# A state-space layer and an FP4 feed-forward layer on one core: x loaded in place, loop buffers laid over used weights, engine lists written out, Silu table loaded first

## The reference

```python
# block 1: linear state space, state of 16, hidden 256
xB = x @ B.T;  xD = x @ D.T
state_t = state_(t-1) @ A.T + xB_t          # a scan over 2048 steps
out = layernorm(states @ C.T + xD) * gamma + beta
x = layernorm(x + out)
# block 2: feed-forward, 256 -> 704 -> 256
q(v): per 16 values, scale = max|v| / 6, v / scale rounded to the FP4 grid, times scale
h = silu(q(x) @ q(w_gate).T) * (q(x) @ q(w_up).T)
x = layernorm(x + q(h) @ q(w_down).T)
```

## Time and profile before

| | |
|---|---|
| median of three runs | 607.63 us |
| the profiled execution | 608.48 us |
| its span in the trace | 606.7 us |
| TensorE busy | 566.4 us (93%) |
| VectorE busy | 511.2 us (84%) |
| GpSimd busy | 494.2 us (81%) |
| ScalarE busy | 473.2 us (78%) |
| DMA | 38.35 MB, mean 63 GB/s |

### The profile page before, as it was taken

The page is one execution under the profiler, slowest core; times in us unless marked ns, Lnnn a source line. Parts: engine busy times, 40 slices in busy tenths (PEclk is TensorE's granted clock), DMA queues, the critical chain, the costliest instruction groups (busy, mean ns, idle before and its releaser), DMA issues.

```text
span 606.7 us, 12733 instructions
## 1 busy us (share of the span) xinstructions
PE 566.4 (93%) x3699; PEld 504.2 (83%) x3699; DVE 511.2 (84%) x1226; ACT 473.2 (78%) x1424; POOL 494.2 (81%) x672
## 2 busy tenths in 40 slices
PE   7986577899999999999999999999999999999974
PEld 6763555799999999999999999999999999999864
DVE  4484124699999999999999999999999999999971
ACT  2663255578888888888888888888888888888763
POOL 3243163789999999999999999999999999998642
PEclk9997676899999999999999999999999999999997
DMA  6653031111112111111111111111111111100001
GB/s 214 261 202 102 2 84 39 33 38 39 56 56 58 55 57 57 56 55 55 55 55 55 55 55 55 55 55 55 55 55 55 55 55 55 55 26 18 18 21 41
DMA packets 46268, 38.35 MB, mean 63 GB/s; under 512 B 7008, under 2 KB 44960, under 8 KB 45216
## 3 DMA queue, kind: packets, MB, share of 16 engines
q1 hardware_dynamic: 46240, 38.00, 20.6%
HBM read 19.50 MB, written 8.39 MB: 46 GB/s over the span
## 4 chain that ended last, share of the span: by engine, by line
PE 85%; DVE 6%; ACT 3%; DMA 2%; issue 2%; SPq 1%; POOL 1%; POOLq 0%; DVEq 0%; ACTq 0%
PE gu L1089 39%; PE turned L1089 18%; PE yb L1089 7%; PE turned L1143 7%; DMA scratch<-in_L_attn_x_dram 2%; PE turned L1110 2%; PE yb L978 1%; PE yb L1100 1%; PE gu L978 1%; PE turned L1154 1%; PE turned L1153 1%; PE grid L919 1%; DVE scratch L858 1%; DVE htLo L887 1%; PE gu L1011 1%
## 5 line engine op out<-in xcount | busy, mean ns | idle before, releaser
L1089 PE MATMUL gu<-wguHi,xtHi 128*128 128x512 f32 (+1 forms) x384 | 152.7, 398 | 0.4 <-DVE xtLo L851 0.2
L1089 PE MATMUL gu<-wguLo,xtHi 128*128 128x512 f32 (+1 forms) x384 | 145.2, 378 | 0.0
L1089 PE MATMUL gu<-wguHi,xtLo 128*128 128x512 f32 (+1 forms) x384 | 145.2, 378 | 0.0
L1089 PE MATMUL turned<-wdHi,htHi 128*128 128x256 f32 x320 | 92.3, 289 | 3.8 <-DVE htLo L887 3.8
L499 POOL TENSOR_TENSOR scratch<-scratch 128x704 f32<-128x704 f32 x64 | 92.2, 1441 | 2.5 <-DVE scratch L872 1.8
L1089 PE MATMUL turned<-wdHi,htLo 128*128 128x256 f32 x320 | 91.8, 287 | 0.0
L1089 PE MATMUL turned<-wdLo,htHi 128*128 128x256 f32 x320 | 90.9, 284 | 0.0
L504 POOL TENSOR_TENSOR scratch<-scratch 128x640 f32<-128x640 f32 x64 | 81.9, 1279 | 9.6 <-DVE scratch L882 9.6
L1089 PEld LDWEIGHTS gu<-wguHi,xtLo 128*128 128x128 f32 x384 | 73.1, 190 | 12.6
L1089 PEld LDWEIGHTS gu<-wguHi,xtHi 128*128 128x128 f32 x384 | 73.3, 191 | 10.3 <-DVE xtLo L851 1.0
L1089 PEld LDWEIGHTS gu<-wguLo,xtHi 128*128 128x128 f32 x384 | 73.3, 191 | 8.7
(11 more groups left out here) (191 smaller groups left out, 1650.8 us busy)
## 6 DMA issues: line engine op xcount, KB each, us to landing
scratch<-in_L_attn_x_dram SPq DMA_DIRECT2D x8, 1024.0 KB, 5.0
xtTile<-xT SPq DMA_DIRECT2D x64, 128.0 KB, 2.3
scratch<-in_L_attn_x_dram SPq DMA_DIRECT2D x64, 128.0 KB, 2.4
out_dram<-scratch SPq DMA_DIRECT2D x64, 128.0 KB, 1.9
stTile<-statesHi SPq DMA_DIRECT2D x128, 8.0 KB, 1.8
stTile<-statesLo SPq DMA_DIRECT2D x64, 8.0 KB, 1.7
scratch<-in_L_ffn_w_down_dram SPq DMA_DIRECT2D x1, 704.0 KB, 6.2
scratch<-in_L_ffn_w_up_dram SPq DMA_DIRECT2D x1, 640.0 KB, 6.0
```

Source lines behind the costliest of these rows:

```text
L1089: ins = nc.tensor.matmul(to, l, r, start=(first and q == 0), stop=(last and q == len(passes) - 1))
```

## The change

The tiles, the operations of the loop and their lags in `run` stay. What changes:

1. `load_x(h)` writes block h into `xT[:, h]`, the place to which the transposes of that block are copied, so that it waits for nothing. All eight are issued in the first list of SyncE, five of them with nothing but DMA issues ahead. `xT` is laid out by block, so that a tile's columns are 1 KB per partition in one piece. A and B are loaded ahead of x.
2. SyncE's order behind the x loads: `tMat`, `cStack`, `qPad`, `load_columns` of tiles 0 to 3, the residual's tiles 0 to 3, then the states of tile 0 (the Hi parts as soon as `states_hi` is done) and of tiles 1 to 3. The waits for all transposes and all `w_lo` are gone.
3. The views over `scratch` get explicit places: what the first tiles need lies over parts of wX and wM that were used, or behind them.
4. Each compute engine's preamble and first six to eight tiles are one written-out list, in which operations of the preamble and of the tiles are interleaved (`FILLED` says where `run` goes on). The waits at the end of the preamble become waits of single operations. `xt_copy(0)` and `xt_copy(28)` move to VectorE. `busy(3)` is gone; `busy(12)` is `busy(10)` with plain matmuls.
5. `w_transposes` uses two PSUM banks in place of three, x transposes from u = 16 use a bank of `grid` in place of `yb`. `mean_square` writes its unread output to PSUM.
6. ScalarE begins with a Silu of one column.

```diff
-        xT = sb("xT", [P, CHUNK, KH, CHUNKS])
+        xT = sb("xT", [P, HALVES, CHUNK, KH, P])
...
             def load_x(h):
-                if h >= 2:
-                    sp.wait_ge(s_xt, 4 * (h - 1))
-                sp.dma_start(xRaw[:, h % 2, :], x_v[h].rearrange("p t d -> p (t d)")).then_inc(s_xload[h % 2], 16)
+                sp.dma_start(xT[:, h, :, :, :].rearrange("p t c k -> p (t c k)"),
+                             x_v[h].rearrange("p t d -> p (t d)")).then_inc(s_xload[h], 16)
...
+            for h in range(4, HALVES):
+                load_x(h)
             sp.dma_start(gamma_b[:, :], gamma.unsqueeze(0).to_broadcast([P, H])).then_inc(s_bcast, 16)
             sp.dma_start(beta_b[:, :], beta.unsqueeze(0).to_broadcast([P, H])).then_inc(s_bcast, 16)
+
+            sp.wait_ge(s_tDiag, 1)
+            sp.wait_ge(s_pwc, POWER_COPIES[LOG_C + 1])
+            for i in range(2, CHUNK, 2):
+                sp.dma_start(tMat[N * i:N * i + N, 0:N * i],
...
-            sp.wait_ge(s_xtc, 4)
+            copied(sp, 3)
             for tile in range(RING):
                 load_columns(0, tile)
+            for tile in range(RING):
+                sp.dma_start(xTile[:, tile, :], x_v[0, :, tile, :]).then_inc(s_ldx[tile], 16)
+            sp.wait_ge(s_sthi, 1)
+            load_states(0, 0, (0, 1))
             sp.wait_ge(s_states, 1)
-            load_states(0, 0)
-            sp.wait_ge(s_xt, 4 * HALVES)
-            sp.wait_ge(s_wlo, len(W_GROUPS))
+            load_states(0, 0, (2,))
+            for tile in range(1, RING):
+                load_states(0, tile)
...
+            act.wait_ge(s_half, 1)
+            nc.scalar.activation(unread[:, :], neg_half[:, :], ACT.Silu)
```

The middle of ScalarE's list and the beginning of GpSimd's:

```diff
+            w_abs(0)
+            xt_copy(6)
+            xt_copy(7)
+            powers(8)
+            t_hi(0, 0)
+            t_hi(0, 1)
+            xt_copy(8)
+            xt_copy(9)
+            w_abs(1)
+            xt_copy(10)
...
+            w_norm(0)
+            w_norm(1)
+            t_lo(0, 0)
+            t_lo(0, 1)
+            w_scale(0)
+            w_scale(1)
```

TensorE's list, of which the parts left out go on in the same way:

```diff
-            pe.wait_ge(s_dc, 32)
-            d_and_c()
-            for u in range(4 * HALVES):
-                x_transposes(u)
-                if u < min(GROUP_AFTER):
-                    busy(3)
...
-            pe.wait_ge(s_xtc, 4 * HALVES)
-            pe.wait_ge(s_states, 1)
-            pe.wait_ge(s_wlo, len(W_GROUPS))
-            pe.wait_ge(s_cstack, 48)
...
+            busy(10)
+            d_and_c()
+            powers(0)
+            powers(1)
+            powers(2)
+            powers(3)
+            powers(4)
+            x_transposes(0)
+            x_transposes(1)
+            powers(5)
+            g_products()
+            x_transposes(2)
...
+            x_transposes(8)
+            x_transposes(9)
+            pair_sums(0)
+            x_transposes(10)
...
+            w_transposes(8)
+            layer(0, 0)
+            w_transposes(9)
+            pair_sums(3)
+            layer(0, 1)
+            chunk_states(1)
+            link(1, 0)
+            layer(0, 2)
+            link(1, 1)
+            link(1, 2)
+            link(1, 3)
+            x_turn(0, 0)
+            layer(0, 3)
+            gu0(0, 0)
...
+            x_turn(0, 3)
+            ffn_down(0, 0)
+            gu0(0, 3)
+            run(pe, [(h_turn, 6), (gu1, 4), (gu2, 4), (x_turn, 3), (layer, 0), (ffn_down, 6), (gu0, 3)], FILLED["pe"])
```

More of the change, by code:

```diff
@@ L264, in ssm_fp4_ffn, with copied, run @@
         PEELED = 2
-        def run(eng, ops, after={}):
+        def copied(eng, u):
+            eng.wait_ge(s_xtc, sum(k not in VECTOR_COPIES for k in range(u + 1)))
+            if min(VECTOR_COPIES) <= u:
+                eng.wait_ge(s_xtcv, sum(k in VECTOR_COPIES for k in range(u + 1)))
+        def run(eng, ops, first):
             last = max(lag for _, lag in ops)
@@ L277, in run @@
                 for i in range(CHUNK):
[L278 to L280 removed]
+                    if CHUNK * h + i >= first:
+                        step(h, i, False)
             with eng.Fori(PEELED, HALVES) as h:
@@ new lines, in _ @@
+            t_hi(0, 0)
[4 more added lines that the diff above has]
+            xt_copy(10)
+            xt_copy(11)
+            powers(9)
+            w_hi(0)
+            xt_copy(12)
+            xt_copy(13)
+            powers(10)
+            xt_copy(14)
+            xt_copy(15)
+            w_hi(1)
+            w_hi(2)
+            w_abs(2)
+            sums_copy(0)
+            w_abs(3)
+            xt_copy(16)
+            xt_copy(17)
+            last_states(0)
@@ new lines, in _ @@
+            xt_copy(18)
+            xt_copy(19)
+            xt_copy(20)
+            xt_copy(21)
+            w_hi(3)
+            xt_copy(22)
+            w_hi(4)
+            xt_copy(23)
+            w_hi(5)
+            xt_copy(24)
+            w_abs(4)
+            w_abs(5)
+            xt_copy(25)
+            xt_copy(26)
+            states_hi(0)
+            xt_copy(27)
+            xt_copy(29)
+            w_hi(6)
+            xt_copy(30)
+            w_hi(7)
+            xt_copy(31)
@@ new lines, in _ @@
+            xt_copy(0)
+            w_max(0)
+            w_recip(0)
+            w_max(1)
+            w_recip(1)
+            w_sum(0)
+            w_grid(0)
+            w_sum(1)
+            w_grid(1)
+            w_max(2)
+            w_lo(0)
+            w_recip(2)
+            w_max(3)
+            w_recip(3)
+            w_lo(1)
+            w_max(4)
+            w_sum(2)
+            w_recip(4)
+            w_grid(2)
+            w_max(5)
+            w_sum(3)
+            link(0, 0)
+            w_grid(3)
@@ new lines, in _ @@
+            link(0, 1)
+            w_recip(5)
+            link(0, 2)
+            w_lo(2)
+            link(0, 3)
+            w_lo(3)
+            link(0, 4)
+            w_lo(4)
+            link(0, 5)
+            w_lo(5)
+            link(0, 6)
+            w_sum(4)
+            w_sum(5)
+            link(0, 7)
+            w_grid(4)
+            w_grid(5)
+            states_lo(0)
+            xt_copy(28)
+            w_lo(6)
+            w_lo(7)
+            w_lo(8)
+            w_lo(9)
@@ new lines, in _ @@
+            link(1, 1)
+            link(1, 2)
+            link(1, 3)
+            x_turn(0, 0)
+            layer(0, 3)
+            gu0(0, 0)
+            link(1, 4)
+            gu1(0, 0)
+            x_turn(0, 1)
+            gu2(0, 0)
+            link(1, 5)
+            layer(0, 4)
+            gu0(0, 1)
+            link(1, 6)
+            gu1(0, 1)
+            link(1, 7)
+            gu2(0, 1)
+            link(1, 8)
+            x_turn(0, 2)
+            layer(0, 5)
+            gu0(0, 2)
```

627 lines of the change are left out of this document (409 added, 218 removed).

## The result

The changed kernel takes 598.58 us (median of four runs, 595.46 to 601.51), the kernel before beside it 608.13: ratio 0.985, 95% interval 0.9813 to 0.9888. Faster was right; the forecast of 593.0 was 5.6 us too low. The profiled execution took 600.9 us; its span is 598.3, against 606.7 before.

A forecast was written before the change was run, and what follows sets the result against it. Idle time and TensorE's clock before T7 were taken as the bound, not work. T7 = 68.5 (34.5 + 34) + 42 = 110.5 in place of 125.98, 15.5 us earlier: 608.48 - 15.5 = 593.0 us, range 579 to 605.

The forecast's parts named there:

- T7: Start of `h_turn(1)` on TensorE, from where TensorE is bound; forecast at 110.5 in place of 125.98, 15.5 us earlier.
- the start: Preamble up to `x_transposes(10)` on TensorE: forecast at about 34.5 us in place of 25.68, 9 us later.
- C: From `x_transposes(10)` to the first `layer`: 34 us taken, bounds 31 to 50, in place of 50.2.
- D: From the first `layer` to T7: 42 us taken, bounds 37 to 50, in place of 50.1.
- The x queue: SyncE's bulk loads at the beginning: 11.1 MB at 378 GB/s from 2.9 us, last byte landing at 32.3 us.
- `xtTile(0)` at 33: First small tile load, queued behind all x: issued near 20 us, landing at 32.3 + 0.13/0.378, say 33.
- ScalarE's arrival: ScalarE reaches `t_hi(0, 0)` in the preamble at 18.6 us and stands until 33, 14.4 us, holding the other engines.
- Silu 0: Second table load, between the first `layer` and T7, gone: 1.28 us, hidden by ScalarE's 4.93 us wait, so 0.
- `busy(3)` 0: Preamble: removing `busy(3)` takes TensorE work from a stage paced by ScalarE's copies; 0, half clock already priced.
- No standstill: Rival: small DMAs pass the x loads, `xtTile(0)` lands at 22, standstill 3 us, total 581.5; chance 0.22.
- The fill gives back: Rival: interleaved lists wait on each other, D takes 46 to 50, total 597 to 601; within the forecast's 0.60.
- Slower: Rival: TensorE stays at half clock until the loop, C 50 and D 50, total 617; chance 0.09.

The follow-up runs named there:

- the next variant: Changed kernel with `tMat` and `load_columns` ahead of x blocks 4 to 7, plus residual tiles 4 to 7 ahead of the state loads: 579.44 us, ratio 0.9527.
- the base run: The changed kernel measured again with nothing altered, beside its variants (also the other profile): 596.25 us, ratio 0.9844 to the kernel before.
- all three edits: Changed kernel with small loads ahead of the bulk, residual tiles 4 to 7 early, `t_hi` and `t_lo` of tiles 0 and 1 later: 573.64 us, ratio 0.945.

## Why the prediction was right, and where it was off

The gain to T7 was put at 15.5 us and is 9.07. The missing 6.4 us split by the prediction's own steps into three: the start 3.4 later than written (37.90 for 34.5), C 1.0 shorter (32.98 for 34), D 4.0 longer (46.03 for 42). So the path to T7 was right and the range held; the start was sized too small, and D lacked a wait.

**The x queue: near, 1.6 us short.** The last byte was to land at 32.3 us. Adding up the windows of after, with the queue served:

```profile
20.00:25.00 5.00, 2.19 (x35) 1.03 (x33) 0.29 (x1) 0.00 (x0) 0.00 (x0) 1.00 1.04 419
25.00:30.00 5.00, 0.00 (x0) 0.00 (x0) 0.00 (x0) 0.00 (x0) 0.00 (x0) 0.59 1.01 419
30.00:33.00 3.00, 0.00 (x0) 0.00 (x0) 0.00 (x0) 0.00 (x0) 0.00 (x0) 0.50 1.11 277
...
33.00:36.65 3.65, 0.00 (x0) 0.00 (x0) 0.00 (x0) 0.00 (x0) 0.00 (x0) 0.50 1.09 259
```

Up to 36.65 us, 313 x 19.68 + 359 x 16.97 = 12.25 MB moved; without the last 3.65 us at 259 it is 11.3 MB by 33. So the 11.1 MB of the estimate were through at about 32.4 if they were served first. Their last load, beta, issued at 16.60, landed 17.3 us later, at 33.9. The rate was not the steady 378 of the estimate, but 313 on average over the first 19.68 us, then 419 until 30 and less after it; that the sum came so near is partly luck. The Trainium skill (DMA: Bandwidth & Descriptors, Bandwidth) gives about 358 GB/s for each core when both cores of an HBM domain stream; here one core read x at 419, and the measurement decides.

**`xtTile(0)` at 33: the step that failed in the start.** The term was 0.13/0.378, 0.3 us behind the last x byte; it measured 2.7 us behind beta, and 4.3 behind the 32.3 of the estimate. The four `xtTile` loads were issued from 26.94 on, not near 20, took 9.7 to 8.4 us and landed at 36.6, 36.8, 37.0 and 37.2; `t_hi` started at 36.65, not 33. Two things stood in the way that the term left out. The eight `qPad` loads, only 64 KB, were ahead of `xtTile` and landed one by one from 33.6 to 36.5, 0.2 us before it. And the engines, as full as before, moved less: from 33 to 36.65 us all 1,064 packets were under 2 KB, at 259 GB/s, where from 25 to 30 nine in ten were larger, at 419. In pieces that small, only the four `xtTile` and four residual loads (1.05 MB together) had that much left to move. Whether `qPad` ahead or the residual beside them held `xtTile` is open; no run took either away.

**ScalarE's arrival and the holding of all engines: right.** At 19.68 for 18.6 (17.60 in the other profile), the wait 16.97 us for 14.4 (19.31). The written sum does not close: 4.5 and five rounds of 0.9 make 9.0 and not 9.6, and four pairs of 2.2 on top 17.8, between what the two profiles show. TensorE's next transposes came 1.25 us behind `t_hi`. Moving the small loads proved the cause: 17 us became 3 (6.4 in the next variant's profile) and the kernel 12 us faster. The sentence that nothing hides the standstill holds.

**C: right in sum, with the clock inside it.** 34 was taken; 33.0 came in one profile and 29.3 (38.16 to 67.45) in the other. The estimate at full clock was 29.5, and the faster execution, at full clock from 45 us on, came to that.

**D: the step that failed most.** "residual tiles and beta are ready ahead (add_beta 0 to 3 stand before the first layer)" looked at four tiles. The list of GpSimd has `add_beta(0, 4)` among the first tiles' operations, and its load stands on SyncE behind the twelve state DMAs of tiles 0 to 3 and four loads of tile 4, issued from 67.6 to 77.8 us: 0.6 us each. With those loads early D is 40.4 and 40.0, between the 36 to 37 that the chain and TensorE's work gave and the 42 taken. The working of TensorE's part was sound; a queue that the step had to be followed through was left out. It is worth 5.7 to 6.1 us, more than the 4.0 by which D came out above the 42.

**The loop, 7.59 a tile and nothing behind T7: right**, 480.72 and 481.39 us. So the layout, the views and the unread outputs cost at most the 0.7 between them behind T7. The two banks for the weights and the two copies on VectorE were not run by themselves.

**Silu 0, `busy(3)` 0: not contradicted.** The Silu was run alone: 606.03 for 606.96, which is 0.9 us and within the 0.3%. That the second table load costs nothing is shown; the first one, of which the prediction says nothing, delayed the first copy by 1.3 us, and the 0.9 us by the medians cannot be told from 0. `busy(3)` was run with the small loads first, where ScalarE's wait hides some of its cost: 585.31 for 584.49.

**The rivals.** "No standstill" did not happen: the queue was in order, as the changed profile's 17 us show, against 3 when the same loads stand ahead. Its number, 581.5, is what the kernel comes near (584.5, then 579.4) when the loads are put so that its premise is true. "The fill gives back", D 46 to 50 and 597 to 601, is what happened (D 46.0, 598.58), though through one late load rather than through lists waiting on each other, and with a start 3.4 us late that it did not have. "Slower", by the clock: half clock after the standstill did appear in both profiles, and in a later stretch of C in the one of the upper group, but C + D was 79, not the 91.5 at which it decides.

## What to carry to other kernels

When transfers are freed from their waits, list everything that stands behind them in the same queue and who needs it first: the small loads for the next step go ahead of the bulk (12 us here), and the next tile's operands ahead of twelve issues of something else (5 us). What the freeing itself is worth lies largely in that queue too: held back, the x loads cost TensorE 1.3 us of waiting for x and about 10 for the small loads behind them. In a written-out engine list, an operation that waits for a late load belongs behind the work that does not need it; but if several such operations follow, moving one only moves the hole (596.56 for 596.25), and the load itself must come earlier.

## What the runs showed of the hardware that was not expected

- One issue can be held up for long when the queue is loaded. Of the four x loads issued from 9.25 us on (6.83 us together), three took 0.43 to 0.47 us each and the second 5.36, from 9.76 to 15.12; in the base run it took 5.59. That alone put `tMat` and all behind it 5 us later. What ends such a hold no row says.
- Small loads behind the bulk are as late as the bulk: `tMat`, issued from 16.9 us, reached TensorE at 34.4 in the kernel with `t_hi` later. The Trainium skill (DMA: Bandwidth & Descriptors, Queues, rings and completion order) has descriptors consumed in ring order on each DMA engine; the trace agrees, with `tMat` at 32.5 to 34.5, `qPad` at 33.6 to 36.5 and `xtTile` at 36.6 to 37.2 in the first profile. Completion is in order only roughly: two of the three `tMat` loads landed before beta (33.9), which was issued ahead of them.
- The same kernel, with the same waits, ran in two groups 5 us apart, told apart by the granted clock of TensorE between 50 and 65 us (0.82, 0.50 and 0.66, or 1.00 throughout). About 4 of the 5 us lie in the span and up to 1 around it, 2.5 to 2.8 us in place of 1.8. What tips it was not found. The version with all three edits has a mean clock of 0.970 to 0.974, and its five runs lie within 1.6 us.
